# A six-layer windowed attention: the queries' inverse norm moved into the exponentials' scale, and the softmax's division moved between two products

## What is computed

```python
q, k, v = split(shift_tokens(x) @ Wqkv[i])          # 16 heads of 64 features
q = q / max(norm(q), 1e-12) * q_scale               # per token and head
k = k / max(norm(k), 1e-12) * k_scale
q = q * cos * scale + rotate_half(q) * sin * scale  # rotary position
k = k * cos / scale + rotate_half(k) * sin / scale
sim = einsum(q, k) * 8                              # windows of 32 queries by 64 keys
attn = softmax(where(mask, -max, sim))
x = (attn @ v) @ Wo[i] + x
x = ffn(layernorm(shift_tokens(x))) + x             # gelu-gated
```

## Time and profile before

| what | value |
|---|---|
| median of three runs | 4082.11 us |
| profiled execution: its own time | 4079.09 us |
| profiled execution: span of the core | 4077.2 us |
| mean granted TensorE clock | 0.983 |
| PE busy | 3769.5 us, 92% |
| DVE busy | 3329.4 us, 82% |
| ACT busy | 3208.0 us, 79% |
| POOL busy | 3370.7 us, 83% |
| chain that ended last, by engine | PE 62%, DVE 22%, issue 8%, ACT 4%, POOL 3% |

### The profile page before, as it was taken

How to read it: one execution, slowest core, us unless ns; L and a number is a source line. 1 busy time by engine, 2 the same in 40 slices (tenths; PEclk the granted TensorE clock), 3 DMA queues, 4 the chain that set the end, 5 groups by cost and what they waited for, 6 DMA issues and landing times.

```text
span 4077.2 us, 163553 instructions
## 1 busy us (share of the span) xinstructions
PE 3769.5 (92%) x61792; PEld 3141.1 (77%) x61792; DVE 3329.4 (82%) x8896; ACT 3208.0 (79%) x11601; POOL 3370.7 (83%) x2461
## 2 busy tenths in 40 slices
PE   7998885999989999989999899999899998999997
PEld 5665664888877888868888778888688887788886
DVE  7998887888878888878888788888788887888885
ACT  6888995888866888848888668888488886688883
POOL 4554445999978999959999779999599997799992
PEclk9999997999999999999999999999999999999999
DMA  3000000111112111112111121111121111111111
GB/s 87 0 0 1 0 0 21 39 39 38 37 37 55 38 38 37 41 36 54 38 37 38 35 56 39 36 39 39 37 54 37 37 39 35 41 38 37 39 39 42
DMA packets 302004, 145.50 MB, mean 36 GB/s; under 512 B 83989, under 2 KB 293779, under 8 KB 301459
## 3 DMA queue, kind: packets, MB, share of 16 engines
q1 hardware_dynamic: 301458, 137.25, 13.9%
HBM read 21.85 MB, written 2.10 MB: 6 GB/s over the span
## 4 chain that ended last, share of the span: by engine, by line
PE 62%; DVE 22%; issue 8%; ACT 4%; POOL 3%; DVEq 1%; SPq 0%; DMA 0%; ACTq 0%; POOLq 0%
PE bank L737 18%; PE bank L848 7%; PE pair L828 7%; PE pair L776 7%; PE bank L730 6%; PE pair L769 5%; PE pair L911 4%; PE bank L797 3%; DVE top L1517 3%; DVE by_sin L1569 3%; DVE norm L1576 2%; DVE qk_parts L1492 2%; DVE top L1593 2%; PE bank L714 2%; DVE prob L1611 2%
## 5 line engine op out<-in xcount | busy, mean ns | idle before, releaser
L1288 POOL TENSOR_TENSOR rnorm<-norm2g,neg_half 128x16 f32<-128x16 f32 x384 | 1118.7, 2913 | 28.0 <-DVE norm2g L1586 22.7
L1280 POOL TENSOR_TENSOR rotated<-by_cos,by_sin 128x512 f32<-128x512 f32 x768 | 994.8, 1295 | 41.9 <-DVE by_sin L1569 41.6
L1116 ACT ACTIVATE pair<-pair,top 128x64 f32<-128x64 f32 x3072 | 895.0, 293 | 82.8 <-DVE top L1593 82.8
L1300 POOL TENSOR_TENSOR rotated<-rotated,rnorm 128x512 f32<-128x512 f32 x768 | 788.4, 1051 | 0.5
L737 PE MATMUL bank<-wqkv_high,xt_high 128*128 128x512 f32 (+1 forms) x1536 | 661.7, 431 | 13.2 <-ACT squares L1107 12.1
L1107 ACT ACTIVATE squares<-bank 128x512 f32<-128x512 f32 x768 | 458.7, 597 | 258.5 <-DVE by_sin L1569 217.3
L1116 ACT ACTIVATION_READ_ACCUMULATOR pair<-pair,top 128x1 f32 x3072 | 654.6, 213 | 0.0
L776 PE MATMUL pair<-qk_t 64*32 64x64 f32 (+1 forms) x18432 | 608.7, 217 | 0.0
L1561 DVE TENSOR_TENSOR by_cos<-bank,rot_cos 128x512 f32<-128x512 f32 x768 | 528.3, 688 | 82.7 <-PE bank L737 45.0
L1593 DVE TENSOR_REDUCE top<-pair 128x4 f32<-128x256 f32 x768 | 325.1, 423 | 279.3 <-PE pair L776 274.1
L1576 DVE TENSOR_REDUCE norm<-squares 128x8 f32<-128x512 f32 x768 | 519.2, 676 | 10.8 <-ACT squares L1107 10.1
(11 more groups left out here) (151 smaller groups left out, 8980.1 us busy)
## 6 DMA issues: line engine op xcount, KB each, us to landing
vmoved<-vout_all SPq DMA_DIRECT2D x1152, 64.0 KB, 2.1
ctx_all<-vout_all SPq DMA_DIRECT2D x384, 64.0 KB, 2.1
wqkv_sb<-in_L_ffn_Wqkv_dram SPq DMA_DIRECT2D x36, 256.0 KB, 3.8
ctx_all<-y SPq DMA_DIRECT2D x48, 128.0 KB
ctx_all<-y SPq DMA_DIRECT2D x48, 127.0 KB
wo_sb<-in_L_ffn_Wo_dram SPq DMA_DIRECT2D x6, 512.0 KB, 10.1
out_dram<-y SPq DMA_DIRECT2D x8, 256.0 KB, 3.5
w_sb<-in_L_ffn_W_dram SPq DMA_DIRECT2D x6, 341.0 KB, 3.3
```

The lines of the kernel that those rows point to most:

```text
L1116: last = nc.scalar.activation(at, at, ACT.Exp, bias=top[jl % 2][:, h:h + 1], accum_out=psum_raw[jl % 2][:, h:h + 1])
L1280: nc.gpsimd.tensor_tensor(rotated[j % 4][:, :, :, :], by_cos[j % 2][:, :, :, :], by_sin[j % 2][:, :, :, :], ALU.add).then_inc(c_rot, 1)
L1288: nc.gpsimd.tensor_tensor(rnorm[slot][:, :, :].rearrange("t g n -> t (g n)"), norm2g[slot][:, :, :].rearrange("t g n -> t (g n)"), neg_hal ...
L1300: nc.gpsimd.tensor_tensor(at, at, rnorm[slot][:, i, :].unsqueeze(2).to_broadcast([P, 2 * HG, DH]), ALU.mult).then_inc(c_unit, 1)
```

## The change

The queries are no longer normalised on POOL. `win_unit` multiplies only the keys' half of the rotated tile (128x256 in place of 128x512). The queries' inverse norm enters later: a softmax over `s * r`, where r is the row's inverse norm and positive, has the maximum `max(s) * r`, so `win_max` writes `-max(s)` to a new tile `peak`, a new operation `win_top` multiplies it by r into `top`, and each exponential gets r as its scale, read from the tile `rnorm` as a column per partition, next to the bias. `rnorm` has four buffers in place of two, because it is read five steps later. On DVE, `win_recip` and `win_scale` move in front of `win_sin`.

```diff
-        rnorm = ring("rnorm", 2, [P, 2, 2 * HG])
+        rnorm = ring("rnorm", 4, [P, 2, 2 * HG])
+        peak = ring("peak", 2, [P, HG])
...
+        c_peak = sem("c_peak")
...
                     for h in range(HG):
                         at = win_ps[jl % 2][:, h // 2, h % 2 * KEYS:(h % 2 + 1) * KEYS]
-                        last = nc.scalar.activation(at, at, ACT.Exp, bias=top[jl % 2][:, h:h + 1], accum_out=psum_raw[jl % 2][:, h:h + 1])
+                        q = 2 * (h % 2) + h // 2
+                        last = nc.scalar.activation(at, at, ACT.Exp, bias=top[jl % 2][:, h:h + 1], scale=rnorm[jl // 2][:, jl % 2, q:q + 1],
+                                                    accum_out=psum_raw[jl % 2][:, h:h + 1])
...
-                        at = rotated[(j - 2) % 4 + i][:, :, :, :].rearrange("t a h d -> t (a h) d")
-                        nc.gpsimd.tensor_tensor(at, at, rnorm[slot][:, i, :].unsqueeze(2).to_broadcast([P, 2 * HG, DH]), ALU.mult).then_inc(c_unit, 1)
+                        at = rotated[(j - 2) % 4 + i][:, 1, :, :]
+                        nc.gpsimd.tensor_tensor(at, at, rnorm[slot][:, i, HG:2 * HG].unsqueeze(2).to_broadcast([P, HG, DH]), ALU.mult).then_inc(c_unit, 1)
...
-                    nc.vector.tensor_reduce(top[slot][:, :].rearrange("q (e i) -> q e i", e=2), win_ps[slot].rearrange("q e (i k) -> q e i k", i=2),
-                                            AX_X, ALU.max, negate=True).then_inc(c_top, 1)
+                    nc.vector.tensor_reduce(peak[slot][:, :].rearrange("q (e i) -> q e i", e=2), win_ps[slot].rearrange("q e (i k) -> q e i k", i=2),
+                                            AX_X, ALU.max, negate=True).then_inc(c_peak, 1)
+
+            def win_top(layer, it, j):
+                if here(it, j, WIN.top):
+                    m = layer * GROUPS + it * STEPS + j - WIN.top
+                    jl = (j - WIN.top) % STEPS
+                    dve.wait_ge(c_peak, m + 1)
+                    nc.vector.tensor_tensor(top[jl % 2][:, :].rearrange("q (e i) -> q e i", e=2), peak[jl % 2][:, :].rearrange("q (e i) -> q e i", e=2),
+                                            rnorm[jl // 2][:, jl % 2, 0:HG].rearrange("q (i e) -> q e i", e=2), ALU.mult).then_inc(c_top, 1)
...
             def win_step(layer, it, j):
                 win_cos(layer, it, j)
-                win_sin(layer, it, j)
                 win_recip(layer, it, j)
                 win_scale(layer, it, j)
+                win_sin(layer, it, j)
                 win_max(layer, it, j)
+                win_top(layer, it, j)
                 win_norms(layer, it, j)
...
                     win_max(layer, ENDED, j)
+                    win_top(layer, ENDED, j)
```

More of the change, by code:

```diff
@@ L1286, in win_rnorm @@
                     pool.wait_ge(c_nrm2g, g + 2)
-                    slot = j // 2 % 2
-                    nc.gpsimd.tensor_tensor(rnorm[slot][:, :, :].rearrange("t g n -> t (g n)"), norm2g[slot][:, :, :].rearrange("t g n -> t (g n)"),
+                    slot = j // 2
+                    nc.gpsimd.tensor_tensor(rnorm[slot][:, :, :].rearrange("t g n -> t (g n)"), norm2g[slot % 2][:, :, :].rearrange("t g n -> t (g n)"),
                                             neg_half[:, :], ALU.pow).then_inc(c_rn, 1)
@@ L1294, in win_unit @@
                     u = layer * UNITS + it * (STEPS // 2) + j // 2 - 1
-                    slot = (j // 2 - 1) % 2
+                    slot = (j // 2 - 1) % 4
                     pool.wait_ge(c_rn, u + 1)
```

## The result

The changed kernel takes 4587.19 us (median of four runs, 4581.41 to 4588.26) against 4082.61 us, a ratio of 1.1235 with a 95% interval of 1.1216 to 1.1255. It is slower, as forecast, but by 505 us in place of 402, and so outside the range of 4350 to 4570 us.

What follows compares the result with a forecast made beforehand. POOL was taken to bound the straight stages at 3.70 us a step; a ring of 4.24 us adds 390 us there and the drains 12, from 4079.1 to 4481 us, 4484 as median; range 4350 to 4570 us.

Steps and rivals of the forecast that it cites:

- The ring: Straight stages: sine product, squares, copies, exponentials, reciprocal, division, next sine product form a loop, 4.19 us, 4.24 with input copy.
- the reciprocal's wait: Sign in the straight stages: reciprocal idle for ACT's exponentials about 0.5 us in nearly each step, over 300 us in total.
- The scale operand: Four exponentials a step on ACT, each about 0.09 us longer for a scale from memory: 0.36 us a step.
- The new multiplication: 128x4 on DVE: 0.17 us plus 0.1, bounds 0.17 to 0.42; costs nothing in the straight stage, lies open in drains.
- What bounded the kernel before: Straight stages: POOL bounds them, 99% busy at 3.69 us a step, with PE 0.2 us behind.
- Rival 1: Straight stages: reciprocal still doesn't wait, POOL falls to 3.2 us, PE leads with 3.49; 3925 us, chance 0.05.
- The clock: TensorE in the straight stages: granted clock stays 1.00 despite 0.75 us gaps; rival of a fall to 1.2 GHz, chance 0.04.
- The other rivals: Straight stages: scale operand free, 4216 us, chance 0.08; slack elsewhere eats the ring, nothing changes, chance 0.02.

Runs made afterwards that it cites:

- The relief alone: Kernel before, with POOL normalising the keys alone and the queries' norm left out: 4081.45 us, ratio 0.9999.
- the run with neither ring nor hold: Changed kernel with the sine product back ahead of reciprocal and division, and `peak` in PSUM: 4159.77 us, ratio 1.0188.

## Why the prediction was wrong, point by point

**The ring: right.** The order on DVE puts the exponentials of one step into the way of the next sine product. Undoing it gains 359 us, or 336 without the hold; doing it alone costs 161 us. The forecast length, 4.19 us, was met term by term by the steps that nothing else disturbs (4.20 and 4.21), and 3.83 without the operand by 3.84. Of the signs that the forecast named, the reciprocal's wait was 194 us in place of over 300, because the hold took its place in DVE's queue; with the peak in PSUM it is 378.

**The scale operand: right in size.** 0.36 us a step was forecast. The exponential grew by 0.09 to 0.10 us, an undisturbed step of the ring by 0.37, and the kernel by 230 us of an expected 261.

**The new multiplication: the step that failed.** "I take 0.17 plus 0.1 [...] In the straight stage I cost it at nothing." Its bounds, 0.17 to 0.42 us, came from the durations of DVE instructions on similar shapes, and all of those have an input in PSUM or one input only. Measured: 0.16 us, or 0.8 to 1.2 us where it is held (1400 to 1880 us), 0.62 on the mean of all, above the upper bound, because with both inputs in SBUF it is held until POOL's addition ends. "It lies beside the squares and hits neither the cosine product nor the exponentials" failed with it. In the held steps from 1400 to 1880 us the cosine product ended 2.8 to 3.6 us after the sine product, where the forecast has 2.4 and the steps with a short multiplication have 2.4 to 2.8, and in most of them the reciprocal, which could have started at about 3.0, stood behind it; and the exponentials began at 1.4 to 1.6 us in place of 1.28. With the peak in PSUM the kernel takes 4496 us, inside the range. The other 91 us are this hold, 76 of them in the straight stages. The timelines laid over each other would have shown the meeting, though not its price: POOL's addition waits for the sine product, POOL is hardly ever idle, and by the forecast's own schedule the multiplication was to run 0.35 to 0.55 us behind the sine product's end. The Trainium skill has the rule ("SBUF — State Buffer", section "Who interferes with whom"): a VectorE instruction with two SBUF inputs and a GpSimd instruction that reads SBUF exclude each other, and the one that comes second waits for the whole of the other. For POOL's additions the traces agree, 67 of 67 and 60 of 60 long ones end with them, and for its multiplications too, 30 of 30. For the power they don't: it reads SBUF as well, runs 2.9 us, and the short ones within it, 42 and 35 in the same windows, took 0.16 us. Here the measurement decides.

**The sum, by runs.** From 4082 the order makes 4243 (+161); relief and a multiplication that isn't held make 4266 (+23); the operand 4496 (+230); the hold 4587 (+91). These four steps come from kernels that differ by one thing each, except the +23, which holds two.

**What bounded the kernel before: wrong, without harm to the forecast.** "POOL bounds the straight stage, PE stands 0.2 us behind it" rested on 99% busy and on a period of POOL's, 3.69 us a step, that equals the stage's mean of 3.70. That mean holds quick first steps, though; in the loop bodies of 29.96 us a step is 3.74 us, and POOL waited. The relief alone gave 0.9999. POOL only follows: its instructions start when DVE's results come, and nearly nobody waits for POOL. What the chain names is PE's work together with a passage through DVE's maxima, norms, cosine, sine and division. The new multiplication lies in it, which fits the 4160 us of the run with neither ring nor hold, since relief and operand alone cost nothing there (4081 and 4084 us); that it explains all of the 78 us is argued, because the bare multiplication was never run by itself. Rival 1 rested on the same error: even without the ring there was no gain to win.

**The clock: right.** With a gap of 0.58 us on the mean in 45 of 46 steps, where 0.75 had been forecast, the granted clock stayed at 1.00 in the stage., on which the forecast of the clock rested, have only a busy share of 85% and no length of a gap; this trace has both. The other rivals fell with it: the operand isn't free, and nothing absorbed the ring.

## What to carry to other kernels

An engine at 99% is a bound only if somebody waits for it; take its load away in an experiment before paying for the relief. Before an instruction that waits is moved ahead of another, write down who waits for that other one: if the list comes back to the thing waited for, the step has become a ring, and each duration in it, however well hidden before, counts in full. A small VectorE instruction with both inputs in SBUF costs, beside GpSimd's additions and multiplications here, what GpSimd's instruction has left to run (not so beside its power); one input in PSUM avoided it.

## What the runs showed of the hardware

- A VectorE `tensor_tensor` of 128x4 with two SBUF inputs took 0.16 us alone or beside GpSimd's power of 128x16, up to 1.26 us beside GpSimd's addition of 128x512, and up to 1.56 us beside its subtraction of 128x682; with one input in PSUM 0.16 us always. The wait is in its duration, not in the idle time ahead of it.
- A second operand from memory on an ACT exponential of 128x64 costs 0.09 to 0.10 us each, four in a row and with accumulator reads between them.
- GpSimd's multiplication by a broadcast operand took 1051 ns for 128x512 and 615 ns for 128x256: half the elements, 59% of the time.
